# Softmax sums spread over the value product, swaps on ScalarE's queue, another score bank, output weights kept on chip: one attention layer and one mixture-of-experts layer on one core

## The reference

```
# attention, 16 heads of 64
q, k, v = split_heads(x @ Wq), split_heads(x @ Wk), split_heads(x @ Wv)
q, k = rope(q), rope(k)                       # (x1,x2) -> (x1*cos-x2*sin, x1*sin+x2*cos)
sim = where(causal, q @ k.T / 8, -inf)
out = softmax(sim) @ v                        # per head
y = concat_heads(out) @ Wo + bo
x = layernorm(x + y)
# mixture of experts: 8 experts of 512, 2 chosen per token
w = softmax(x @ gate_w.T + expert_bias); top2, normalized
out = sum_e w[e] * (gelu(x @ w_up[e].T) @ w_down[e].T)
x = layernorm(layernorm(out) + x)
```

## Time and profile before

| what | value |
| --- | --- |
| time, median of 3 runs | 805.8 us |
| profiled execution, its own time | 798.51 us |
| its span | 796.7 us |
| TensorE busy | 755.9 us (95%) |
| VectorE busy | 667.4 us (84%) |
| ScalarE busy | 592.2 us (74%) |
| GpSimd busy | 572.0 us (72%) |
| mean granted TensorE clock | 0.997 |
| DMA queue of SyncE, share of the 16 engines' span | 53.8% |

### The profile page before, as it was taken

How to read it: one execution, slowest core, us unless ns; L and a number is a source line. 1 busy time by engine, 2 the same in 40 slices (tenths; PEclk the granted TensorE clock), 3 DMA queues, 4 the chain that set the end, 5 groups by cost and what they waited for, 6 DMA issues and landing times.

```text
span 796.7 us, 20539 instructions
## 1 busy us (share of the span) xinstructions
PE 755.9 (95%) x5763; PEld 535.0 (67%) x5763; DVE 667.4 (84%) x2514; ACT 592.2 (74%) x1678; POOL 572.0 (72%) x701
## 2 busy tenths in 40 slices
PE   8899999999999999999999989999998899999995
PEld 4455666666666566666666656666656579999995
DVE  6688888999899879998999899989987974235997
ACT  3688878878878777877887768777877756565677
POOL 3686767558765877677768886976786266989983
PEclk9999999999999999999999999999999999999998
DMA  4576666456755566556555655565557667434525
GB/s 152 188 224 200 214 203 201 165 191 197 227 180 174 174 200 195 188 180 210 175 186 191 194 173 186 186 199 173 177 179 225 222 193 207 109 85 125 163 90 163
DMA packets 110719, 144.66 MB, mean 182 GB/s; under 512 B 13392, under 2 KB 86352, under 8 KB 110608
## 3 DMA queue, kind: packets, MB, share of 16 engines
q1 hardware_dynamic: 106240, 134.49, 53.8%
q0 software_dynamic: 4224, 8.72, 3.3%
q10 hardware_dynamic: 144, 0.13, 0.1%
HBM read 61.42 MB, written 45.17 MB: 134 GB/s over the span
## 4 chain that ended last, share of the span: by engine, by line
PE 67%; POOL 13%; DVE 8%; issue 7%; DMA 3%; ACT 1%; SPq 0%; DVEq 0%; POOLq 0%; ACTq 0%
PE AO L1109 15%; PE S_all L1068 14%; PE TB L1089 9%; PE AO L1129 5%; PE S_all L1256 4%; POOL yrows L956 4%; PE TB L1269 2%; POOL shared L973 2%; PE AO L1269 2%; DVE Sm L1609 2%; DMA qk<-shared 2%; DVE x_acc L1630 1%; PE TB L1000 1%; POOL shared L722 1%; PE TB L998 1%
## 5 line engine op out<-in xcount | busy, mean ns | idle before, releaser
L1376 ACT ACTIVATE Pr_all<-Sm,nmax 128x512 f32<-128x512 f32 (+3 forms) x512 | 281.8, 563 | 23.7 <-DVE nmax L1609 22.9
L1609 DVE CUSTOM_DVE_ANT_0 Sm<-S_all,causal 128x512 f32<-128x512 f32 (+3 forms) x512 | 223.0, 482 | 46.0 <-PE S_all L1068 45.9
L1068 PE MATMUL S_all<-qk 64*128 64x512 f32 (+3 forms) x1024 | 169.8, 446 | 10.9 <-DVE nmax L1609 8.6
L717 POOL TENSOR_TENSOR qk<-shared,qk 128x512 f32<-128x512 f32 x64 | 81.9, 1280 | 129.6 <-DMA qk<-shared 119.9
L1109 PE MATMUL AO<-PT,shared 128*64 128x128 f32 x1008 | 149.6, 438 | 13.1 <-issue 12.7
L1386 ACT ACTIVATE PT<-TB 128x768 f32<-128x768 f32 x189 | 107.8, 605 | 61.2 <-PE TB L1089 61.2
L1630 DVE SCALAR_TENSOR_TENSOR x_acc<-AO,rinv,x_acc 128x128 f32<-128x128 f32 x504 | 141.7, 344 | 3.5 <-POOL x_acc L769 1.3
L1068 PEld LDWEIGHTS S_all<-qk 64*128 64x128 f32 x1024 | 79.7, 187 | 82.6 <-issue 56.9
L1089 PE MATMUL TB<-ident,Pr_all 128*128 128x128 f32 x764 | 109.2, 279 | 3.6 <-ACT PT L1386 3.1
L1089 PEld LDWEIGHTS TB<-ident,Pr_all 128*128 128x128 f32 x764 | 82.0, 141 | 44.4 <-issue 40.6
L1109 PEld LDWEIGHTS AO<-PT,shared 128*64 128x64 f32 x1008 | 66.5, 136 | 61.1 <-issue 30.9
(11 more groups left out here) (335 smaller groups left out, 1459.0 us busy)
## 6 DMA issues: line engine op xcount, KB each, us to landing
turns<-turned_pr SPq DMA_DIRECT2D x63, 512.0 KB
PT<-turns SPq DMA_DIRECT2D x252, 128.0 KB
qk<-shared SPq DMA_DIRECT2D x124, 256.0 KB
wo<-in_wo SPq DMA_DIRECT2D x64, 64.0 KB, 3.1
PT<-yrows SPq DMA_DIRECT2D x7, 512.0 KB, 4.3
w_tile<-in_wup SPq DMA_DIRECT2D x10, 256.0 KB, 3.5
xt<-xrows SPq DMA_DIRECT2D x32, 65.0 KB, 2.7
x_acc<-in_x SPq DMA_DIRECT2D x8, 256.0 KB, 3.4
```

The lines of the kernel that those rows point to most:

```text
L717: nc.gpsimd.tensor_tensor(qT[p][:, :], q_cos, qT[p][:, :], ALU.add).then_inc(q_ready, 1)
L1068: nc.tensor.matmul(SB[2 * (group % 2) + h][:, at:at + (qb + 1) * P], qT[p][half, qb * P:qb * P + P], kT[p][half, 0:(qb + 1) * P], start=Tr ...
L1376: nc.scalar.activation(Pr[j][:, 0:n], Sm[j], ACT.Exp, bias=nmax[:, j:j + 1], scale=-1.0, accum_out=rsum[p][:, h * QB + qb:h * QB + qb + 1] ...
L1609: nc.vector.tensor_tensor_reduce(out=Sm[j], in0=SB[2 * (group % 2) + h][:, at:at + n], in1=causal[:, T - n:T], scale=-0.125, scalar=HUGE, ...
```

## The change

It has these parts, all of them in the attention:

1. **Sums.** VectorE's 1/rsum (128 rows x 8) is transposed by TensorE into bank SB[0] (`turn_sums`), copied by VectorE to 8 rows x 128 (`take_norms`), stored to memory by SyncE and loaded back by two DMAs that repeat a row of 512 over 64 partitions each (`spread_norms`). VectorE multiplies the values product with it while it copies it to OT (`norm_o`). `copy_o` of ScalarE goes.
2. **Output projection.** Since OT is normalized, both heads are multiplied at once with 128 rows of the array: 4 matmuls in the place of 8, and 8 pairs are summed up in bank OB. `scale_y` goes, except for the very last unit; `add_y` adds the bank to x_acc once for each batch. The call stands behind the scores of group 2 now.
3. **Score banks.** Group 2 of the scores goes to TB, group 1 of the transposes to SB[0] and SB[1], the later value projections to SB[2].
4. **Swaps.** The two swap DMAs are issued by ScalarE, at the start of the next unit, behind the exponentials of group 2.
5. **Weights.** Wo is loaded once; six of the eight pairs' rows stay in w_tile, two in wo. The weights of experts 6 and 7 are loaded later, since their place holds the spread sums until then.

The core of the diff, line groups in the order of the file:

```diff
+        def spread_of(u):
+            if u < PAIRS:
+                e = E - 2 + u % 2
+                return wdown[:, e * IB:e * IB + IB, :].rearrange("p a c -> p (a c)")
+            return hT[u % 2][:, :]
+        def score_bank(group, h):
+            return TB[:, h, :] if group == 2 else SB[2 * group + h]
+        sums_bank = SB[0][0:BLK, 0:P]
...
+            def spread_norms(u, p):
+                sp.wait_ge(inverted, 2 * u + 2)
+                wait(sp, norms_in, 32 * (u - 1))
+                sp.dma_start(norms[p * BLK:p * BLK + BLK, :], norms_t).then_inc(norms_stored, 16)
+                sp.wait_ge(norms_stored, 16 * (u + 1))
+                wait(sp, o_ready, u - 1)
...
+                for h in range(2):
+                    sp.dma_start(spread_of(u)[D * h:D * h + D, :],
+                                 norms[p * BLK + QB * h:p * BLK + QB * h + QB, :].rearrange("(o q) t -> o (q t)", o=1).to_broadcast([D, T])).then_inc(norms_in, 16)
...
+            def turn_sums(u, p):
+                pe.wait_ge(inverted, 2 * u + 1)
+                pe.wait_ge(maxed, BLK * (u + 1) + DONE_BY[0])
+                nc.tensor.transpose(sums_bank, rinv, ident[:, :]).then_inc(sums_turned, 1)
...
                 for i in range(QB):
-                    for h in range(2):
-                        half = slice(D * h, D * h + D)
-                        last = nc.tensor.matmul(y_bank(u)[h][:, i * P:i * P + P], OT[p][half, i * P:i * P + P],
-                                                wo[p][half, :], start=True, stop=True)
+                    last = nc.tensor.matmul(y_bank[:, i * P:i * P + P], OT[p][:, i * P:i * P + P], wo_of(u),
+                                            start=(first and i == 0), stop=last_pair, skip_group_check=True)
...
                 score(u, p, 0)
-                if u >= 2:
-                    project_out(u - 2, p)
...
                 score(u, p, 1)
-                pe.wait_ge(maxed, BLK * u + DONE_BY[0])
+                    pe.wait_ge(maxed, BLK * u)
+                    wait(pe, pt_ready, 2 * (u - 1))
+                    pe.wait_ge(q_read, min(u + 2, UNITS))
                 score(u, p, 2)
                 if not first:
+                    turn_sums(u - 1, 1 - p)
+                if u >= 2:
+                    project_out(u - 2, p)
+                if not first:
                     transpose(u - 1, 1 - p, 1)
...
-                if u >= 2:
-                    copy_o(u - 2, p)
                 if not first:
                     for j in range(FIRST_OF[2], BLK):
                         exp(u - 1, 1 - p, j)
+                if 2 <= u < UNITS - 1:
+                    swap(u + 1, 1 - p)
...
+            def take_norms(u):
+                dve.wait_ge(sums_turned, u + 1)
+                wait(dve, norms_stored, 16 * u)
+                nc.vector.tensor_copy(norms_t, sums_bank).then_inc(inverted, 1)
+            def norm_o(u, p):
+                dve.wait_ge(pv_done, u + 1)
+                dve.wait_ge(norms_in, 32 * (u + 1))
+                wait(dve, y_done, u - 1)
+                nc.vector.tensor_tensor(OT[p][:, :], o_bank(u), spread_of(u), ALU.mult).then_inc(o_ready, 1)
+            def add_y(b):
+                dve.wait_ge(y_done, min(PAIRS * (b + 1), UNITS - 1))
+                dve.wait_ge(x_set, b + 1)
+                rows = x_acc[:, b * QB:b * QB + QB, :].rearrange("p a c -> p (a c)")
+                nc.vector.tensor_tensor(rows, y_bank, rows, ALU.add).then_inc(y_read, 1)
...
+                if u >= 2:
+                    norm_o(u - 2, p)
+                if not first:
+                    invert(u - 1, 1 - p)
                 mask_max(u, 0)
                 mask_max(u, 1)
-                if u >= 2:
-                    scale_y(u - 2)
-                for j in range(FIRST_OF[1], FIRST_OF[2]):
+                if not first:
+                    take_norms(u - 1)
+                for j in range(FIRST_OF[1], BLK):
                     mask_max(u, j)
```

196 lines of the change are left out of this document (112 added, 84 removed).

## The result

The kernel after takes 882.5 us (median of 4 runs, 875.8 to 885.5), the kernel before 806.6 on the same chip: 1.093 times as long, 95% interval 1.086 to 1.100. Forecast were 812.7, at most 832. The direction was right, the size was off by a factor of ten.

A forecast was written before the change was run, and what follows sets the result against it. TensorE's chain was taken as the bound, 9.17 us a plain unit. Terms summed to +6.9 us: 805.4 from the profiled 798.5, and 812.7 us with 7.3 carried over; range 806 to 821, for 8 in 10 797 to 832.

The forecast's parts named there:

- The plain unit: Undisturbed attention unit, set by TensorE: 9.17 us before, about 9.47 after, +0.30 a unit, +15.9 us over 53 units.
- The path's terms: TensorE's longer unit +15.9, maxima +2.5, values-product waits -13.5, start -3, 8 units +2.4, last two units +0.6, last division -1.
- The output projection gets no shorter: TensorE: half as many instructions, each twice as long, still 0.89 us; costed at nothing, -0.1 to +0.1 us a unit.
- rival D: Output projection's 8 instructions take 0.45 us, half the time: 28 us saved, 785 us; chance 0.03.
- The waits before the values product go: TensorE's 17 waits, 11.8 us, vanish, with 0.1 us of slow start each: -13.5 us (-10 to -17).
- the first of the two reasons: On SyncE, loads of the turned probabilities no longer stand behind late swaps.
- the prediction's second reason: VectorE turns its part of the probabilities about 1 us earlier.
- The waits for maxima, 6.6 + 2.5 us and 0.1 in each unit: TensorE's 9 waits for VectorE, 6.6 us, stay and grow 2.5 (0 to +5); the sums' transpose waits about 0.1 a unit.
- The start, -3 us: Kernel start: the first swap leaves about 1.7 us sooner on ScalarE, and unit 2 follows: -3 us (0 to -4).
- The swaps on ScalarE, +1.5 us: ScalarE stands still until GpSimd's k is ready, and this lateness reaches TensorE: +1.5 us (0 to +6).
- Rival C: Sums or swaps late in most units: 837 us with 4.8 us swaps, 829 with sums 0.3 late; chance 0.13.
- The round trip of the sums, 0: Store and loads between take_norms and norm_o: back at 9.0 us, wanted at 9.6, so hidden; 0 for the usual unit.

The follow-up runs named there:

- the path alone: Kernel after, without the sums' store and two loads (norm_o multiplies by the cosine table) and with swaps issued by SyncE again: 810.8 us, ratio 1.007.
- without the trip: Kernel after, without the sums' store, two spread loads and their waits; norm_o multiplies by the cosine table: 825.7 us, ratio 1.027.
- small turned loads: Kernel before with swaps on ScalarE, and from the third unit on four turned loads of 32 KB each in place of 128: 802.4 us, ratio 0.998.
- `norm_o` later and no trip: Kernel after without the sums' store and loads, swaps on SyncE, norm_o behind the two maxima of group 0: 829.4 us, ratio 1.031.

## Why the prediction was wrong, step by step

- *The plain unit.* Forecast 9.47, measured 9.42. The path's terms without the swaps and the trip (15.9 + 2.5 - 13.5 - 3 + 2.4 + 0.6 - 1) make +3.9 us; the run with the path alone shows 0.7%, some 6 us. That the sums agree is partly luck: -13.5 and -3 were argued in the first place from the swaps' leaving SyncE, and in this run they are on SyncE.
- *The output projection gets no shorter.* Right; rival D is out.
- *The waits before the values product go.* From 11.8 to 3.1 us. The size is right, the first of the two reasons is not. With the swaps alone moved the wait stayed as it was (whole span, as the next figures):

```profile
PE AO L1099 <- issue: 12.0, 17, 1.9
```

  With the path alone, the swaps on SyncE, it is 5.6 us in 6 times. So most of it went with the rest of the change; the prediction's second reason, that VectorE turns its part sooner, fits, and no run tests it alone.
- *The waits for maxima, 6.6 + 2.5 us and 0.1 in each unit.* With the path alone they are 22.2 us in units 9 to 61, where these terms make 14.4. Too small, by some 8 us.
- *The start, -3 us.* Wrong in sign. Unit 9 starts at 99.4 us before, at 101.6 with the swaps alone moved, at 104.3 without the trip, and the +0.3 a unit that was forecast explains 2.4 us at most.
- *The swaps on ScalarE, +1.5 us.* Wrong: 16 us here, 28 alone. I had looked for the cost in ScalarE's time and lateness. The issues in fact cost ScalarE nothing: in this piece of its timeline after, the first swap is issued while exponentials run, and the next one starts as the one before it ends:

```profile
439.13 0.52 ACT L1444 ACTIVATE Pr_all<-Sm,nmax 128x256 f32<-128x256 f32 x1
439.23 0.47 ACTq L1515 DMA_DIRECT2D qk<-shared  x1
...
439.62 0.52 ACT L1444 ACTIVATE Pr_all<-Sm,nmax 128x256 f32<-128x256 f32 x1
```

  The lateness was real: where GpSimd's k is late, ScalarE stands still at the swap. Behind its issue, ScalarE then stood idle 31.5 us in 16 times with the swaps alone moved, 23.8 in 12 without the trip; with the swaps on SyncE, before and with the path alone, no wait there ends at an issue. A row from the waits of the run with the swaps alone:

```profile
ACT Pr_all L1366 <- issue: 22.6, 9, 3.2
```

  With small turned loads it is 11.3 us in 6 times and no loss is left, so this wait is at least in part an effect of the slow swap and not its cause. The cause is what one queue had given for nothing: swap first, turned loads behind it. Rival C had this mechanism, with 4.8 us for the swap and 837 us for the time; the run with the swaps alone gave 832 at 3.8 us plus the issues. I gave it 0.13 because at medians both rounds had slack; but my median of 3.1 us was that of the 64 KB loads of Wo, not of a swap with other loads beside it. The Trainium skill (DMA: Bandwidth & Descriptors, Issuing engines are not separate DMA queues) says that all queues run on the same 16 engines; the rows agree (3.14 us with the turned loads queued behind the swap, 3.78 with them on the other queue), and I had read it only as "no gain", not as a transfer that now shares the engines with another.
- *The round trip of the sums, 0.* This is the step that failed: 53 of the 76 us. Two things were wrong in it. The way is longer than my 5.9 us from `take_norms`: two issues stand between the landings, not one (0.50 and 0.59, with the last landing counted from the second), and the landings in the kernel after are 2.6 and 3.7 us from the start of their issue, so 0.3 + 2.4 + 1.1 + 3.1 = 6.9 us, where rival C said that it decides from 6.5. And I took SyncE as free when the sums were ready. I listed what is queued behind a wait for TensorE, VectorE and ScalarE, but did not add up SyncE's own round: two landings waited for in order, 2.6 to 3.1 and 3.5, and 3.2 us of issues make 9.3 to 9.8.
- *Lateness adds to the next unit.* Rival C's 829 took 0.3 us a unit. With the round above the unit's 9.42, a late unit is not made good before the next one: `norm_o` is 0.8 us late in the median and up to 5.5.
- *The clock.* Not in the prediction. After some of the long waits TensorE starts at its lower level. In the 6.2 us up to 420.5 it was busy for 2.48, and its last wait was 3.7 us; behind it the chain and the window show:

```profile
420.88 1.71 PE AO L1173 x8
422.59 1.71 PE S_all L1128 x8
```
```profile
420.50:426.70 6.20, 6.20 (x25) 5.62 (x26) 3.55 (x15) 2.49 (x7) 0.58 (x2) 0.52 0.52 145
430.00:439.40 9.40, 9.21 (x64) 6.10 (x62) 7.92 (x27) 6.95 (x22) 5.20 (x5) 1.00 0.62 197
```

  The granted clock is 0.52 there, half speed, and 1.00 in the plain unit after it; the same blocks take 1.71 in place of 0.89. Of the 53 units 9 to 61, 8 have a mean granted clock of 0.59 to 0.76 from `turn_sums` to the values product, behind waits of 2.5 to 5.3 us. That piece takes 5.8 to 7.3 us in them, where the median of all is 4.6, 14 us more in sum. It fits the mean clock of all these units, 0.97 against 1.00. Not every wait of that length does it: behind one of 2.8 us and one of 2.6 the clock is 1.00. This follows from the waits and is part of the trip's price.

No version here that computes everything beats the kernel before. Without the trip the rest of the change still costs 2.7%, and with the swaps back on SyncE 0.7%.

## What to carry to other kernels

A queue that waits for a landing is an engine like the others: write down its round, with each landing and each issue in order, and compare it with the unit before adding a second wait. A row of a DMA's duration holds only beside what ran when it was taken; moving a transfer to another queue takes away the order that kept others behind it. When two single remedies bring little, try them together before giving up the cause.

## What I had not expected of the hardware

- A second queue slowed the swap, from 3.14 to 3.78 us from issue to use, and that was 28 us in the whole; with a quarter of the other queue's bytes it was 2.82.
- Issues on ScalarE left no gap where work was queued ahead of and behind them on the engine (the swaps among the exponentials at 439 us), and about 1 us a unit where the next instruction is waited for (59.9 us in 62 units).
- One DMA of 256 KB with an outer dimension of 2 in place of two of 128 KB: the time went from 873 to 1153 us. On ScalarE's queue the one load had 2 packets of 4 bytes where the two had 32, and took 8.3 us in place of 3.3.
- After a wait the output projection took 1.16 us in place of 0.89 though the granted clock was 1.00 on average (100 to 690 us of the run with `norm_o` later and no trip). All of it is at the first instruction, 0.38 us in place of 0.27 and overlapped by nothing ahead; the others start 0.11 us apart in both.
